# First batch's thresholds ahead of the latents' low parts, its transposed sum ahead of the folds, and a scatter that finishes token tile by token tile

## The reference

```python
# 1: learned adjacency from the latents ctx (4 x 256 x 64)
sim = (ctx Wq^T)(ctx Wk^T)^T / 16                    # 256 x 256 per batch
threshold = top_k(sim, 76)[..., -1]                  # the 76th largest of each row
A = sigmoid(sim) * (sim >= threshold)
x = x + tanh(g0) * ((1 - gamma) * layernorm(x) + gamma * (A + A^T) / 2)
# 2: 16 blocks of hidden units, the 4 best by a router: gelu(x W1) * mask, then W2
# 3: latent attention: 16 heads over the latents, queries with rotary positions
# 4: mixture of experts: 32 experts, 4 per token, each takes at most 40 tokens,
#    out[token] += weight * expert(x[token]); and a shared expert; x = x + tanh(g3) * (...)
```

## Time and profile before

| | |
|---|---|
| median of three runs | 465.26 us |
| profiled execution, its own time | 466.26 us |
| its span on the core | 464.5 us |
| PE busy | 432.4 us (93%) |
| DVE busy | 301.3 us (65%) |
| ACT busy | 252.4 us (54%) |
| POOL busy | 193.9 us (42%) |

### The profile page before, as it was taken

How to read it: one execution, slowest core, us unless ns; L and a number is a source line. 1 busy time by engine, 2 the same in 40 slices (tenths; PEclk the granted TensorE clock), 3 DMA queues, 4 the chain that set the end, 5 groups by cost and what they waited for, 6 DMA issues and landing times. The chain is left out here.

```text
span 464.5 us, 8843 instructions
## 1 busy us (share of the span) xinstructions
PE 432.4 (93%) x2723; PEld 276.3 (59%) x2723; DVE 301.3 (65%) x880; ACT 252.4 (54%) x629; POOL 193.9 (42%) x195
## 2 busy tenths in 40 slices
PE   5895999989988999999999999999999998889996
PEld 2584787777744555556555555555568773644476
DVE  3979799965247757667676667757744558446613
ACT  3593336364344776767677766776666252145500
POOL 3441314040434556565456655556644425444000
PEclk9996899999999999999999999999999999999999
DMA  7743000000204343443324334212200599789202
GB/s 249 218 97 102 1 1 2 1 1 2 68 0 97 78 107 76 94 122 68 98 71 102 90 76 104 57 44 52 64 23 2 148 308 305 210 203 244 65 30 92
DMA packets 61448, 43.81 MB, mean 94 GB/s; under 512 B 22955, under 2 KB 54502, under 8 KB 61414
## 3 DMA queue, kind: packets, MB, share of 16 engines
q1 hardware_dynamic: 60646, 41.04, 33.2%
q0 software_dynamic: 768, 2.36, 2.6%
HBM read 27.25 MB, written 2.23 MB: 63 GB/s over the span
## 5 line engine op out<-in xcount | busy, mean ns | idle before, releaser
L1206 POOL TENSOR_TENSOR W1T<-W1T,inv 128x512 f32<-128x512 f32 x64 | 66.5, 1039 | 77.4 <-DVE inv L1261 77.4
L1150 ACT ACTIVATE W1T<-ps,low 128x256 f32<-128x256 f32 x128 | 59.5, 470 | 30.8 <-DVE low L1255 30.8
L276 POOL TENSOR_TENSOR rot<-rot 128x512 f32<-128x512 f32 x48 | 61.0, 1270 | 28.7 <-DMA rot<-rot 28.7
L1255 DVE TENSOR_REDUCE low<-ps 128x2 f32<-128x512 f32 x64 | 44.1, 688 | 39.2 <-PE ps L1065 38.6
L1158 ACT ACTIVATE W2T<-ps 128x512 f32<-128x512 f32 x64 | 38.2, 597 | 7.2 <-PE ps L1073 5.2
L1073 PE MATMUL ps<-ident,W1T 128*128 128x128 f32 x256 | 41.1, 283 | 0.9 <-POOL W1T L1206 0.8
L1073 PEld LDWEIGHTS ps<-ident,W1T 128*128 128x128 f32 x256 | 27.8, 141 | 23.7 <-issue 20.3
L256 DVE TENSOR_TENSOR rot<-ps,sinq 128x512 f32<-128x512 f32 x48 | 33.1, 690 | 13.4 <-PE ps L243 11.2
L243 PE MATMUL ps<-XH,CH 128*128 128x512 f16 x96 | 36.4, 379 | 0.9 <-DVE XL L862 0.9
L243 PE MATMUL ps<-XL,CH 128*128 128x512 f16 x96 | 36.4, 379 | 0.0
L243 PE MATMUL ps<-XH,CL 128*128 128x512 f16 x96 | 36.4, 379 | 0.0
(11 more groups left out here) (247 smaller groups left out, 863.5 us busy)
## 6 DMA issues: line engine op xcount, KB each, us to landing
rot<-rot SPq DMA_DIRECT2D x64, 128.0 KB, 2.3
rot<-rot SPq DMA_DIRECT2D x64, 64.0 KB, 2.0
EGU<-in_L_ffn_W_gate_dram SPq DMA_DIRECT2D x8, 384.0 KB, 5.9
EGU<-in_L_ffn_W_up_dram SPq DMA_DIRECT2D x8, 384.0 KB, 5.8
ED<-in_L_ffn_W_down_dram SPq DMA_DIRECT2D x8, 384.0 KB, 6.1
rot<-in_L_ffn_W_dram SPq DMA_DIRECT2D x2, 1024.0 KB, 8.4
WQ<-in_L_xattn_Wq_dram SPq DMA_DIRECT2D x8, 256.0 KB, 2.9
WO<-in_L_xattn_Wo_dram SPq DMA_DIRECT2D x8, 256.0 KB, 3.1
```

The lines of the kernel that those rows point to most:

```text
L276: pool.tensor_tensor(g.RO[:, n, x, :], g.RO[:, n, x, :], g.TC[x][:, :], ALU.add).then_inc(g.sum_ok, 1)
L1150: e = act.activation(PB[t % 2][:, h, :], g.ps[:, SC + t % 2, h * S:(h + 1) * S], ACT.Exp, bias=low[:, t % 2, h:h + 1], scale=-1.0, accum_o ...
L1206: pool.tensor_tensor(PB[t % 2][:, :, :], PB[t % 2][:, :, :], inv[:, t % 2, :].unsqueeze(2).broadcast_to([P, 2, S]), ALU.mult).then_inc(nor ...
L1255: dve.tensor_reduce(low[:, t % 2, :], g.ps[:, SC + t % 2, :].rearrange("p (h s) -> p h s", h=2), AX.X, ALU.min).then_inc(low_ok, 1)
```

## The change

In the opening, four things move; no instruction is added or taken away.
- DVE forms batch 0's `A` before `kv_rest()`, not after it.
- In the rounds of the next batch `first` comes one round earlier (after r = 1), the norm's apply after r = 2 in batch 1 and r = 3 later (before: 4), `route` after r = 5 in batch 1 (before and later: 6).
- PE runs `symmetric(0)` ahead of all six folds.
- ACT makes batch 0's square root in the middle of the folds, after the third.

In the end part, the first stretch of the scatter takes slot tiles 0 to 6 for token tiles 0 to 4 alone (70 matmuls, after pairs below EARLY = 12); after `d_pack[1]` each token tile is finished in turn, so that tiles 5 to 7 have all their 20 matmuls there. The last token tile has a bank of its own (4), and waits for ACT to have emptied it (`hp_ok`). DVE waits for tiles 6 and 7 singly, and the output goes out in five DMAs, the last two of one tile each.

```diff
         pe.wait_ge(id_ok, 2)
+        symmetric(0)
         for k in range(FOLDS):
-            if k == FOLDS // 2:
-                symmetric(0)
             fold(k)
...
         for k in range(FOLDS):
             fold(k)
+            if k == FOLDS // 2 - 1:
+                norm_root(act, g, n1, 0)
         for b in range(B):
-            norm_root(act, g, n1, b)
+            if b >= 1:
+                norm_root(act, g, n1, b)
...
-                if b == 0 and r == 9:
-                    kv_rest()
...
-                if b >= 1 and r == 2:
+                if b >= 1 and r == 1:
                     first(b - 1)
-                if b >= 1 and r == 4:
+                if b >= 1 and r == (2 if b == 1 else 3):
                     norm_inverse(dve, g, n1, b - 1)
                     norm_apply(dve, g, n1, b - 1)
...
-                if b >= 1 and r == 6:
+                if b >= 1 and r == (5 if b == 1 else 6):
                     route(b - 1)
...
+            if b == 0:
+                kv_rest()
...
-        FULL = TILES_S - 2
+        FULL, AHEAD_T = TILES_S - 3, 5
...
-                for b in range(B):
-                    sp.wait_ge(fin_ok, 2 * b + 2)
-                    sp.dma_start(out_v[:, 2 * b:2 * b + 2, :], g.X[:, 2 * b:2 * b + 2, :]).then_inc(stored, 16)
+                out_parts = ((0, 2), (2, 4), (4, 6), (6, 7), (7, 8))
+                for first, end in out_parts:
+                    sp.wait_ge(fin_ok, end)
+                    sp.dma_start(out_v[:, first:end, :], g.X[:, first:end, :]).then_inc(stored, 16)
...
-                for t in range(NT):
+                for t in range(AHEAD_T):
                     for n in range(FULL):
                         scatter(t, n)
                 pe.wait_ge(d_pack[1], N_PACK[1])
                 for t in range(NT):
-                    for n in range(FULL, TILES_S):
+                    if t == NT - 1:
+                        pe.wait_ge(hp_ok, PAIRED)
+                    for n in range(FULL if t < AHEAD_T else 0, TILES_S):
                         mm = scatter(t, n)
                     mm.then_inc(acc_ps, 1)
...
+                for t in range(NT):
+                    dve.wait_ge(acc_ps, t + 1 if t >= NT - 2 else t // 2 * 2 + 2)
+                    dve.scalar_tensor_tensor(out=g.X[:, t, :], in0=acc(t), scalar=fin_gate[:, 0:1],
+                                             in1=g.X[:, t, :], op0=ALU.mult, op1=ALU.add).then_inc(fin_ok, 1)
```

More of the change, by code:

```diff
@@ L1374, in stage_moe @@
             :, TILES_S * T:TILES_S * (T + 2 * D)].rearrange("p (n a d) -> p n a d", n=TILES_S, a=2)
-        FULL = TILES_S - 2
+        FULL, AHEAD_T = TILES_S - 3, 5
+        acc = lambda t: g.ps[:, LASTB, 0:D] if t == NT - 1 else g.ps[:, ACC + t // 2, D * (t % 2):D * (t % 2) + D]
         EARLY = -(-FULL * P // (2 * CAP))
@@ L1408, in stage_moe @@
         KEYB, LISTB, SLOTB = 6, 5, 7
-        XTB, GU, HTB, Y, SHB, ACC = 0, 2, 4, 6, 4, 0
+        XTB, GU, HTB, Y, SHB, ACC, LASTB = 0, 2, 4, 6, 4, 0, 4
         pair_of = lambda n: (EPT * n + count(n) - 1) // 2
@@ L1465, in _ @@
                     pack(q)
-                for b in range(B):
-                    sp.wait_ge(fin_ok, 2 * b + 2)
-                    sp.dma_start(out_v[:, 2 * b:2 * b + 2, :], g.X[:, 2 * b:2 * b + 2, :]).then_inc(stored, 16)
-                sp.wait_ge(stored, 16 * (1 + B))
+                out_parts = ((0, 2), (2, 4), (4, 6), (6, 7), (7, 8))
+                for first, end in out_parts:
+                    sp.wait_ge(fin_ok, end)
+                    sp.dma_start(out_v[:, first:end, :], g.X[:, first:end, :]).then_inc(stored, 16)
+                sp.wait_ge(stored, 16 * (1 + len(out_parts)))
             @block.gpsimd
@@ L1679, in _ @@
                 down(PAIRED - 1)
-                acc = lambda t: half_bank(ACC, t)
                 def scatter(t, n):
@@ L1684, in scatter @@
                         mm = pe.matmul(acc(t), STT[:, n, t * P:(t + 1) * P], YP[:, n, part, :],
-                                       start=(t % 2 == 0 and n == 0 and part == 0),
+                                       start=((t % 2 == 0 or t == NT - 1) and n == 0 and part == 0),
                                        stop=(n == TILES_S - 1 and part == 1), skip_group_check=True)
```

## The result

The changed kernel took 463.19 us (median of 7 runs, 461.59 to 463.52), the kernel before 465.11 us (7 runs beside them, 464.53 to 467.84). The ratio, which compares means and not medians, is 0.9939, with a 95% interval of 0.9920 to 0.9959, so the change makes the kernel about 2.8 us faster (1.9 to 3.7; the two medians lie 1.9 apart). That is the forecast direction, but only half of the 5.4 us forecast, and the median lies 0.9 us above the top of the stated range. In the profiled execution the span is 461.3 us, 3.2 less than the 464.5 of before.

What follows compares the result with a forecast made beforehand. The prediction took PE, full nearly everywhere, to bound the kernel, with a hole and low clock in the opening. Opening -3.9 and end -1.5 gave -5.4 us: 459.9 us from 465.26, range 457.0 to 462.3.

Steps and rivals of the forecast that it cites:

- DVE before the first norm: Opening: A fits into DVE's idle 1.60 us and the norm moves up in the rounds, so XN comes 3.67 us earlier.
- PE and the folds: Opening: with the sum ahead of the folds, PE turns XN at 37.3 us, 3.5 earlier, and the hole is gone.
- The slip of 0.67 us: Opening: the chain of fold copies, low parts and last fold comes 0.67 us later, between nothing and 1.9.
- The clock: Opening: without the long hole the granted clock stays at 1.00, worth 3.94 us; first mask at 43.1 us, 7.4 earlier.
- the one hole of 4.12 us: Opening: PE idles before DVE's first XN; the hole costs its 4.12 us and another 3.94 for the clock.
- The clock rival: Opening: clock falls all the same, low 39.3 to 49.6 us; DVE no bound; total -3.8, 461.5 us; chance 0.12.
- DVE becomes the bound: Batches 1 to 3: PE waits for DVE's A, slowed beside POOL's products, leaving a shift of -3.9 us.
- both races of batch 2 and 3: DVE's A(2), A(3) against POOL's second products: both lost -2.6, one lost -3.9, none -5.2 us.
- the shift of 3.9: Opening's gain at the fourth batch's sum, the middle case with one race lost: 3.9 us earlier.
- The attention stage passes a shift on: Attention stage between opening and end: its loads and products follow semaphores, so the opening's shift passes through unchanged.
- The end: Scatter and output: wait of 0.92 us goes, one addition behind PE, 1.37 us less, output 0.1 less; together -1.5.
- The sum: Whole kernel: opening -3.9 and end -1.5 give -5.4 us, so 459.9 us; forecast chance 0.50.

Runs made afterwards that it cites:

- short filler: Changed kernel plus six matmuls of the identity that nobody reads, in PE's gap before fold 4: 459.84 us, ratio 0.9888 to the kernel before.
- before with a filler: Kernel before the change plus sixteen unread identity matmuls behind the last fold, in PE's hole: 462.26 us, ratio 0.9937.
- end alone: Kernel before's opening orders of PE, ACT and DVE with the changed end part: 463.84 us, ratio 0.9959 to the kernel before.
- eight tiles ahead: Changed kernel with the scatter's first stretch as before (all token tiles, old pair limit), keeping own bank and five output DMAs: 463.29 us, ratio 0.9962.
- sum among the folds: Changed kernel with PE's and ACT's opening order put back (symmetric(0) between the fold halves, root after the last fold copy): 463.43 us, ratio 0.9953.
- twelve fillers: Changed kernel plus twelve unread identity matmuls behind fold 3 and five behind the first turn of XN: 459.89 us, ratio 0.9878.
- apply one round earlier: Changed kernel with the second norm's apply after r = 7 instead of r = 8 in batches 2 and 3: 460.51 us, ratio 0.9895.
- opening-alone kernel: Changed opening with the kernel before's end (scatter in one piece, four output DMAs): 464.04 us, ratio 0.9976 to the kernel before.
- the four with fillers: Changed kernel with 12 and 5, with 6, or with 6 and 2 plus the earlier apply; kernel before with 16: 459.89, 459.84, 457.73, 462.26 us.

## Why the prediction came out as it did

- *DVE before the first norm: right.* A stands in DVE's idle time at 26.80, the wait there shrinks from 1.60 to 0.99. `first(0)` runs at 32.82 (32.7 forecast), XN's apply at 36.43, 3.54 earlier (3.67).
- *PE and the folds: right in time, misread in effect.* The slip of 0.67 us in the chain of fold copies was forecast, and ACT's first copy came at 32.61 (32.65). XN's turn came at 37.82 for 37.3. The same slip makes the wait before fold 4 grow from 0.82 to 1.59 us, and this gap the prediction did not work out. XN is turned 0.5 us later than forecast because the last folds already run at the low clock (L161 and L165 take 0.48 and 1.12 us for 0.33 and 0.65); in the same order at full clock, with the short filler, it comes at 36.88.
- *The clock: wrong, and this is the step that failed.* The prediction put the fall down to the one hole of 4.12 us, took its absence as enough ("no wait longer than some 1.5 us is left") and booked the whole 3.94. Nothing of it came: the clock fell all the same, 3 us earlier than before, behind a wait of 1.59 with short matmuls around it, and stayed low as long, 10.2 us. The clock rival (chance 0.12) describes the result, though it had the low stretch from 39.3 and not from 36.3: second sum forecast at 53.1, measured 52.41; its total of 461.5 is 1.7 too low for a reason of the next point. The Trainium skill, TensorE: Matmul & The Clock Gate, section "A second HAM failure mode: psum-queue depth-cycling", tells of a kernel in which PE was idle for short times between groups of matmuls, and so often that the clock went to and fro between its two levels. The traces here agree in so far as the longest waits ahead of a fall were as short as 1.59 and 2.04 us in two of the changed orders; that it was their number no run here shows. The price itself was right (3.87 measured in before with a filler), and with six fillers in the gap the clock holds, and the forecast's sums and time come out within 0.5 us.
- *DVE becomes the bound: right, and for the rival too.* The forecast has both races of batch 2 and 3 at stake and takes one as lost. Both were lost: A(2) and A(3) took 1.87 each and PE waited 1.24 and 1.25. Each cost PE's lead 1.3 and 1.1 us and not the 1.8 that the prediction reckoned, as one of A's two instructions got through ahead of POOL. So where the clock held, in the kernel with the short filler, the shift of 3.9 came out partly by luck: two small losses (2.4 together) in place of one large one (2.3). The clock rival had taken it that DVE would be no bound any more and kept 2.3 us; but the waits came, as POOL's products follow PE and keep meeting DVE. So of 3.0 us at the second sum 0.6 are left at the fourth, 1.0 at the end of the opening. The rule of the Trainium skill that the prediction named (SBUF — State Buffer, section "SBUF: two separate sides") agrees in both directions: whoever comes second waits, DVE with 1.87 for 0.86, POOL with 1.55 for 1.27.
- *The attention stage passes a shift on: right* (1.02 before, 1.01 behind it). The routing does not: PE's lead falls by 1.5 us in the low stretch and grows by 1.9 behind it, where PE waits for gathered rows. How much the routing and the experts add or take differs from one profiled execution to the next, with no order in it: of the lead behind the attention stage they took 0.5 (end alone), 0.7 (eight tiles ahead), 0.9 (sum among the folds) and 1.6 us (twelve fillers), and added 0.4 (changed kernel), 0.6 (short filler, before with a filler) and 1.0 (apply one round earlier); in the two others they changed it by 0.1. So single executions compare to about 1 us only, and the medians and means decide.
- *The end: right.* No wait ahead of the scatter or inside it, one addition behind it, 1.31 us less for 1.37, and the stored output 0.4 to 0.5 less for 0.1.
- *The sum.* Forecast 3.9 + 1.5. Measured in the profiled execution: 1.0 of the opening, 0.4 of the routing, 1.3 + 0.5 of the end, 3.2 together. Of the 2.9 that the opening lacks, the short filler gives back about 2.4 in the comparison of ratios (0.9888 against 0.9939), and 3.4 at the fourth sum of the profiled executions (93.98 for 97.69, less 0.3 of earlier start).

That the seven runs of the changed kernel spread over 1.9 us fits the clock as well: four with a mean granted clock of 0.982 took 463.2 to 463.5 us, three with 0.985 or 0.993 took 461.6 to 462.1. Half speed for 10.2 us in the opening and for some 7 us in the routing is what 0.982 amounts to. That the short runs had a short stretch in the opening, like the 6.8 us of the opening-alone kernel, is inferred: only the profiled one shows where it lay.

What stays open: why the clock falls in this place of the opening, why the low stretch begins at 36.3 in one execution and at 37.4 or 38.6 in others with the same instructions there and lasts 10.2 or 6.8 us, and what brings a low stretch in the routing. Between 372 and 385 us the profiled executions of the changed kernel and of the four with fillers have one, before with a filler among them (0.83 in 375 to 385 us). The end alone, the sum among the folds and the twelve fillers have one of some 3.4 us at 406 to 411. Before, the opening alone, the apply one round earlier and the eight tiles ahead have none; so it is no matter of the changed order alone. Nor is it thin work: PE of the changed kernel is busy for 0.79, 0.94 and 1.00 of the three microseconds from 375 to 378, and the clock falls at 377.6. Nothing was tried on it.

## What to carry to other kernels

Removing the longest wait of PE need not keep its clock: a prediction that books the clock needs a run that shows it held. Where PE's work is thin and cannot be filled with real work, a handful of matmuls into a free bank is a cheap test; here six in a gap of 1.59 us did not delay the next fold and gave about 2.4 us. When one stage is moved, lay the windows of GpSimd's products beside the VectorE instructions that were seen to stretch (here the thresholding with two SBUF inputs and the norm's apply) again; one round of order decided 2 us. And do not count on a shift passing unchanged through a stage where PE waits for a DMA.

## What the runs showed of the hardware

- The granted clock fell at a longest wait of 1.59 us (changed kernel) and of 2.04 us (sum among the folds), and held in the same code with 1.50 us of fillers in the gap. It did not fall at waits of 2.17 us (ending at 13.66) and 1.78 us (ending at 388.22) of before.
- Once low in the opening it stayed low for 6.8 or 10.2 us, though PE's longest wait in the changed kernel's stretch was 0.69 us; in the routing it fell with PE busy 94% and more, for 6.8 us.
- Beside a product of GpSimd, one SCALAR_TENSOR_TENSOR of VectorE with two SBUF inputs took up to 1.48 us for 0.48. A pair of its TENSOR_SCALARs with one SBUF input took 1.49 us for 0.73, while the MAX8 and MATCH_REPLACE8 rows beside the next ones kept their 0.74 and 0.41 us.
